# Four-layer fp32 attention and FFN kernel on one core: five engine queues in another order, and weight-piece waits on the last products

## The reference, cut to what matters

```python
x = x + L0_xattn(layernorm(x), ctx)      # softmax(q k^T) of the context with itself, then tokens times it
x = L0_ffn(x)                            # residual + ternary-weight FFN, int8 activations, hidden 1024, silu gate
x = x + L1_xattn(layernorm(x), ctx)      # 16 heads of 128, 8 key/value heads, Wo
x = x + L1_ffn(layernorm(x))             # fp8-rounded weights, inner 768, silu(gate) * up, then down
```

## Time and profile before

| what | us |
|---|---|
| median of three runs | 320.16 (319.19 to 320.66) |
| the profiled execution, whole | 319.45 |
| its span, first to last instruction | 317.4 |
| around the span | 2.05 |
| mean granted TensorE clock, of full speed | 0.993 |

### The profile page before, as it was taken

How to read it: one execution, slowest core, us unless ns; L and a number is a source line. 1 busy time by engine, 2 the same in 40 slices (tenths; PEclk the granted TensorE clock), 3 DMA queues, 4 the chain that set the end, 5 groups by cost and what they waited for, 6 DMA issues and landing times.

```text
span 317.4 us, 6401 instructions
## 1 busy us (share of the span) xinstructions
PE 294.9 (93%) x1981; PEld 258.8 (82%) x1992; DVE 252.2 (79%) x713; ACT 258.5 (81%) x607; POOL 217.9 (69%) x290
## 2 busy tenths in 40 slices
PE   3676999999999999999989999999999999999994
PEld 2465566889988987899779989889999998989784
DVE  3789698989888789888889788897877595766674
ACT  0869796489999989999997897788899998975350
POOL 3786663566887788797877897878897696772001
PEclk9999799999999999999999999999999999999999
DMA  7994602002046867678637566687665466200201
GB/s 219 380 350 135 176 0 68 1 1 76 5 81 179 245 168 199 165 209 202 180 88 207 150 179 162 165 221 203 147 188 151 116 197 200 69 2 0 68 1 66
DMA packets 54609, 44.59 MB, mean 140 GB/s; under 512 B 11696, under 2 KB 45104, under 8 KB 54576
## 3 DMA queue, kind: packets, MB, share of 16 engines
q1 hardware_dynamic: 54016, 43.93, 49.1%
q10 hardware_dynamic: 560, 0.26, 0.3%
HBM read 27.01 MB, written 15.20 MB: 133 GB/s over the span
## 4 chain that ended last, share of the span: by engine, by line
PE 21%; ACT 15%; POOL 8%; issue 5%; DVE 1%; ACTq 0%; POOLq 0%; DVEq 0%
PE pb L2015 14%; PE pb L2278 4%; ACT sm L980 4%; POOL tp_lo L666 4%; ACT pT_hi L992 3%; PE pb L2312 2%; POOL xn L588 1%; ACT sm L998 1%; ACT L980 1%; POOL sm L661 1%; ACT L1019 1%; ACT fuse L1019 1%; ACT q_hi L975 1%; ACT oT_hi L1004 1%; POOL rstd L582 1%
## 5 line engine op out<-in xcount | busy, mean ns | idle before, releaser
L666 POOL TENSOR_TENSOR tp_lo<-tp,pT_hi 128x512 fp32r<-128x512 f32 x54 | 69.2, 1297 | 20.9 <-ACT pT_hi L992 20.8
L980 ACT ACTIVATE sm<-sm,smin 128x256 f32<-128x256 f32 x128 | 63.6, 503 | 1.1 <-DVE smin L1563 0.7
L1563 DVE CUSTOM_DVE_ANT_0 sm<-pb,mask_all 128x256 f32<-128x256 f32 x128 | 47.5, 419 | 4.0 <-PE pb L2015 3.6
L1580 DVE STREAM_TRANSPOSE blocks<-sm 128x1024 f32<-128x1024 f32 x27 | 33.5, 1240 | 7.0 <-DMA block_room<-blocks 6.1
L2015 PE MATMUL pb<-ctx_hi,q_hi 128*128 128x256 f32 x128 | 37.8, 295 | 0.5 <-DVE q_lo L1550 0.4
L2015 PE MATMUL pb<-xT_hi,m_hi 128*128 128x256 f32 x128 | 37.2, 291 | 0.1
L2015 PE MATMUL pb<-n_hi,oT_hi 128*128 128x256 f32 x128 | 37.1, 290 | 0.1
L2015 PE MATMUL pb<-xT_hi,m_lo 128*128 128x256 f32 x128 | 36.2, 283 | 0.0
L2015 PE MATMUL pb<-xT_lo,m_hi 128*128 128x256 f32 x128 | 36.2, 283 | 0.0
L2015 PE MATMUL pb<-ctx_hi,q_lo 128*128 128x256 f32 x128 | 36.2, 282 | 0.0
L2015 PE MATMUL pb<-ctx_lo,q_hi 128*128 128x256 f32 x128 | 36.1, 282 | 0.0
(11 more groups left out here) (195 smaller groups left out, 946.4 us busy)
## 6 DMA issues: line engine op xcount, KB each, us to landing
block_room<-blocks SPq DMA_DIRECT2D x108, 128.0 KB, 2.5
tp<-block_room SPq DMA_DIRECT2D x54, 256.0 KB, 3.1
w_raw<-in_w SPq DMA_DIRECT2D x4, 576.0 KB, 4.2
wraw<-in_wgvT SPq DMA_DIRECT2D x4, 512.0 KB, 7.4
wraw<-in_woutT SPq DMA_DIRECT2D x2, 512.0 KB, 10.6
out<-xb SPq DMA_DIRECT2D x4, 256.0 KB, 2.2
xa<-in_x SPq DMA_DIRECT2D x3, 256.0 KB, 4.6
xb<-in_ctxT SPq DMA_DIRECT2D x2, 256.0 KB, 6.1
```

The lines of the kernel that those rows point to most:

```text
L666: g.tensor_tensor(tp_lo[:, z, c, :], tp[:, z, c, :], as_f32(pT_hi[:, c, :]), ALU.subtract).then_inc(pT_lo_pool, 1)
L980: a.activation(sm[:, n % 2, k, :], sm[:, n % 2, k, :], ACT.Exp, bias=smin[:, n % 2, k:k + 1], scale=-1.0, accum_out=ssum[:, n % 2, k:k + 1 ...
L1563: v.tensor_tensor_reduce(out=sm[:, n % 2, k, :], in0=bank(passing_bank("s", 2 * n + h))[:, (k % 2) * S:(k % 2 + 1) * S], in1=mask_all[:, b ...
L1580: v.transpose(blocks[:].rearrange("p g k b -> p k g b"), sm[:, n % 2, :, :].rearrange("p k (g b) -> p k g b", b=32)).then_inc(blocks_done, 1)
```

## The change

The set of calls on each queue is the same before and after; only their order differs (and the banks in `PASSING`, rewritten to match), beside one edit of waits in `down`. The core of the diff, queue by queue:

```diff
@@ SP @@
             rows(2)
+            gate_value(1)
             rows(3)
             gate_value(0)
             gate_value(2)
-            gate_value(1)
             gate_value(3)
             contexts(1)
             hidden_out(0)
+            raw(5)
             raw(0)
+            scales()
             norm_weight()
+            raw(4)
             mask_bytes()
-            raw(4)
-            raw(5)
+            raw(3)
             raw(6)
+            hidden_out(1)
             raw(1)
-            hidden_out(1)
-            raw(3)
             raw(8)
...
             blocks_read(19)
-            eighth(3)
-            scales()
             blocks_read(20)
@@ POOL @@
             outputs_split(0)
-            ternary_out(5)
             integers(0)
             integers(1)
+            ternary_out(5)
             rows3(0)
...
-            normalise(21)
             rows3(3)
             probs_low(18, 0)
             probs_low(18, 1)
+            normalise(21)
             rows4(1)
...
             probs_low(29, 1)
+            eighths_out(14)
             normalise(31)
-            rows4(2)
             eighths(15)
             eighths_out(15)
+            rows4(2)
             rows4(3)
             output(2)
@@ ACT @@
+            context_high(0)
             projected1(0)
-            context_high(0)
             values_high(0)
+            sums(0)
             rows1(0)
             exps1(0)
             projected1(1)
-            sums(0)
             sums(1)
...
             probs(10, 1)
             outputs(9)
             silu(6)
+            gate_copy(7, 1)
             queries(15)
-            gate_copy(7, 1)
-            normalise(13)
-            silu(7)
             outputs(10)
             probs(11, 0)
             exps(14, 0)
...
+            queries(16)
             probs(12, 0)
-            queries(16)
             probs(12, 1)
+            silu(7)
             queries(17)
             normalise(15)
             exps(16, 0)
...
             probs(31, 0)
             probs(31, 1)
+            fuse_high(3)
+            gate4_silu(5)
             outputs(31)
             fuse_high(4)
-            gate4_silu(5)
@@ DVE @@
             centred(0)
-            inverse1(2)
             added1(1)
-            ternary(3)
             scaled(0)
             weight_sums(1)
+            inverse1(2)
+            ternary(3)
             second_stats(1)
@@ PE @@
             def down(c, n):
                 h, i = divmod(c, KI)
                 pe.wait_ge(f_lo_done, c + 1)
+                if c < KI:
+                    pe.wait_ge(w8_done, -(-(2 * KD * INNER + (i + 1) * D) // PIECE))
                 if c == 0 and n == 0:
-                    pe.wait_ge(w8_done, B * EIGHTS)
...
             gate_half(0, 0)
             gate_half(0, 1)
-            gate_half(1, 0)
+            mix(2)
             value_half(0, 0)
...
             attn_out(30, 1)
+            down(2, 1)
             attn_out(31, 0)
             attn_out(31, 1)
+            down(3, 1)
+            rows4(2)
             up4(5)
-            rows4(2)
-            down(3, 1)
             down(0, 0)
```

More of the change, by code:

```diff
@@ L752, in _ @@
             normalise(9)
+            probs_low(7, 0)
             eighths(3)
             eighths_out(3)
-            probs_low(7, 0)
             probs_low(7, 1)
+            eighths(4)
+            probs_low(8, 0)
             normalise(10)
-            probs_low(8, 0)
             probs_low(8, 1)
@@ L763, in _ @@
             probs_low(9, 0)
-            eighths(4)
             eighths_out(4)
+            probs_low(9, 1)
             normalise(12)
-            probs_low(9, 1)
             eighths(5)
@@ L778, in _ @@
             eighths_out(6)
+            normalise(15)
             probs_low(12, 0)
@@ L781, in _ @@
             eighths(7)
-            normalise(15)
+            eighths_out(7)
             probs_low(13, 0)
@@ L836, in _ @@
             normalise(27)
+            eighths(14)
             probs_low(25, 0)
@@ L1112, in _ @@
             exps(2, 1)
-            normalise(1)
+            fused_queries(7)
             outputs(0)
@@ L1116, in _ @@
             probs(1, 1)
-            rounded(2)
+            normalise(2)
+            exps(3, 0)
             queries(4)
-            normalise(2)
+            exps(3, 1)
+            probs(2, 0)
             rounded(3)
-            exps(3, 0)
-            probs(2, 0)
-            exps(3, 1)
+            outputs(1)
             probs(2, 1)
+            queries(5)
+            normalise(3)
+            gate_copy(4, 0)
             exps(4, 0)
-            queries(5)
             exps(4, 1)
-            outputs(1)
-            normalise(3)
+            outputs(2)
             normalise(4)
-            gate_copy(4, 0)
-            gate_copy(4, 1)
             exps(5, 0)
@@ L1135, in _ @@
             queries(6)
+            normalise(5)
+            gate_copy(4, 1)
             silu(4)
-            normalise(5)
-            outputs(2)
             gate_copy(5, 0)
@@ L1141, in _ @@
             queries(7)
-            gate_copy(5, 1)
             probs(3, 1)
+            rows3(1)
             exps(6, 0)
-            rows3(1)
             exps(6, 1)
             outputs(3)
+            probs(4, 0)
             normalise(6)
-            probs(4, 0)
+            exps(7, 0)
+            queries(8)
+            exps(7, 1)
             probs(4, 1)
-            queries(8)
-            exps(7, 0)
-            exps(7, 1)
             normalise(7)
             queries(9)
+            gate_copy(5, 1)
             exps(8, 0)
@@ L1199, in _ @@
             probs(10, 0)
+            normalise(13)
             probs(10, 1)
@@ L1223, in _ @@
             probs(13, 0)
+            exps(16, 1)
             probs(13, 1)
-            exps(16, 1)
+            outputs(12)
+            exps(17, 0)
+            queries(18)
             normalise(16)
-            queries(18)
-            exps(17, 0)
-            outputs(12)
+            outputs(13)
+            probs(14, 0)
             exps(17, 1)
-            probs(14, 0)
             probs(14, 1)
-            outputs(13)
             normalise(17)
@@ L1300, in _ @@
             exps(26, 1)
+            gate4_copy(2)
             gate4_silu(0)
+            probs(23, 0)
+            outputs(22)
+            gate4_silu(1)
+            queries(28)
             normalise(26)
-            queries(28)
-            gate4_copy(2)
-            probs(23, 0)
-            gate4_silu(1)
-            outputs(22)
+            probs(23, 1)
             gate4_silu(2)
-            probs(23, 1)
             exps(27, 0)
             exps(27, 1)
+            queries(29)
+            fuse_high(0)
             probs(24, 0)
@@ L1314, in _ @@
             probs(24, 1)
-            fuse_high(0)
+            gate4_copy(3)
             exps(28, 0)
-            queries(29)
             exps(28, 1)
-            gate4_copy(3)
             normalise(27)
-            normalise(28)
             probs(25, 0)
@@ L1324, in _ @@
             queries(30)
+            normalise(28)
             outputs(24)
@@ L1327, in _ @@
             exps(29, 1)
-            gate4_silu(3)
             probs(26, 0)
-            outputs(25)
             probs(26, 1)
             normalise(29)
+            gate4_silu(3)
+            outputs(25)
             exps(30, 0)
-            exps(30, 1)
+            queries(31)
             probs(27, 0)
             probs(27, 1)
-            queries(31)
+            outputs(26)
+            exps(30, 1)
+            gate4_copy(4)
+            fuse_high(1)
             normalise(30)
-            outputs(26)
-            gate4_copy(4)
+            probs(28, 0)
+            fuse_high(2)
+            probs(28, 1)
+            gate4_copy(5)
             outputs(27)
-            probs(28, 0)
-            probs(28, 1)
             gate4_silu(4)
-            fuse_high(1)
-            fuse_high(2)
-            gate4_copy(5)
             probs(29, 0)
@@ L1355, in _ @@
             normalise(31)
-            fuse_high(3)
             outputs(29)
@@ L1973, in _ @@
             probs_low(30, 1)
+            eighths(15)
             outputs_low(29)
@@ L2322, in _ @@
             rows1(1)
+            rows1(2)
             probs(0)
@@ L2328, in _ @@
             project1(3)
-            turn_kv(0)
+            energy(2)
             probs(1)
-            energy(2)
             mix(1)
             energy(3)
+            turn_kv(0)
             turn_kv(1)
-            rows1(2)
+            integers(0)
             turn_kv(2)
+            probs(2)
+            weight_sum(1)
             turn_kv(3)
-            integers(0)
-            weight_sum(1)
-            probs(2)
-            mix(2)
             gate_half(0, 0)
             gate_half(0, 1)
-            gate_half(1, 0)
+            mix(2)
             value_half(0, 0)
@@ L2396, in _ @@
             fuse_qk(6)
+            turn_queries(7)
+            queries(2)
+            fuse_vo(7)
             fuse_qk(7)
@@ L2418, in _ @@
```

(39 more changed lines are left out.)

628 lines of the change are left out of this document (313 added, 315 removed), and 49 rows, old and new, of the table PASSING.

## The result

The kernel after takes **322.01 us** (median of 12 runs, 320.26 to 325.70) against 320.11 for the kernel before beside it (12 runs, 318.66 to 320.88): ratio **1.0061**, 95% interval 1.0037 to 1.0086. It is slower by 0.6%. The forecast was 318.3, faster by 0.6%; the range 314.8 to 322.8 holds the time, the direction is wrong. The profiled execution took 322.79 us, 320.8 of it span. Medians in this document are of all runs, ratios and the counts of runs by clock only of those that are not slow: the one of 325.70 us here is slow, and so are one of 417 and one of 487 us among the experiments.

The account below looks back on a forecast made before the run. PE, busy 93%, was taken as the bound, leaving only its 22.5 us of idle time to win. Terms -0.3 - 0.9 - 1.0 + 0.3 = -1.9 us, from the median 320.16, gave 318.3 us; range 314.8 to 322.8.

Parts of the forecast that it names:

- Waits of `down`: Lower-half `down` products wait for 12 to 16 weight pieces, not all 16; priced 0, ends -0.2 to +1 us.
- First table load: At the start, ACT's table load runs under PE's first products, so `qk` starts 1.3 us earlier, near 7.5 us.
- Loads: Early `scales()` delays `hidden_out(1)` by 1 to 2 us, taking back the table's gain: net -0.3, ends -1.3 and +1.5.
- the larger gain: Rival, 315 us: table load not taken back, no half-speed stretch, loop saves half a microsecond, -5 us; chance 0.13.
- Gate halves: `gate_half(0, 0)` and `(0, 1)` fill PE's 1.78 us hole before `mix(2)`: -0.9 us, ends -1.8 and 0.
- `silu(7)`: Leaving the chain before PE's `tp_lo` wait at 162.21 us: -1.0; its second visit with two more table loads: +0.3.
- Small moves: Some 300 small order moves, not priced one by one: taken as 0, ends -2 to +4 us.
- the broken hand-off of `tp_lo`: Rival, 323 us: POOL's later `normalise` turns PE's 8 waits for `tp_lo` into 16, +4.8 us; chance 0.21.

Follow-up runs that it names:

- late before: Orders of the kernel after up to about 66 us, but `scales()` left late, those of the kernel before behind, with `down`'s piece waits: 319.58 us, 0.9990.
- late after: The kernel after with one call moved, `scales()` back to its late place ahead of `blocks_read(20)`: 319.14 us, 0.9991.
- part 1: The kernel before with only the edit of `down`'s waits: 320.06 us, 1.0013.
- the kernel of part 3: The kernel before with one call moved, `context_high(0)` first on ScalarE, ahead of `projected1(0)`: 318.12 us, 0.9943.
- a badly cut experiment: Two kernels joining the orders of before and after at about 66 us: early before with late after 323.68 us, 1.0116; early after with late before 319.58, 0.9990.
- the last kernel of part 9: The kernel before with `context_high(0)` first on ScalarE and the first two gate halves ahead of `mix(2)`, in banks drained early: 318.04 us, 0.9947.

## Why the prediction was wrong

The runs give the change a ledger, in ratios to before. The early table load: 0.9943. The rest of the early order, without `scales()`: the kernels with late before (0.9990) and with late after (0.9991) both stand 0.5% above it, the waits of `down` included. The late order, some 300 moves: those two differ by 0.01%, so nothing, within 0.3% (their early calls are the same but for a few at the cut). `scales()` early: 0.9991 to 1.0061, plus 0.7%. Sum: -0.6 + 0.5 + 0.0 + 0.7 = +0.6%. It closes because each step is the difference of two measured kernels, some timed at different times, so each is good to about 0.3%.

Against the forecast, in us by these ratios: table load and loads -0.3 forecast, +0.4 measured (+1.5 by the medians); the rest of the early order with the gate halves -0.9, measured +1.5; the late order with `silu(7)` -0.7, measured 0. Two steps failed, the price of the loads and the nothing put for the early small moves, beside the gate halves that won nothing.

- *Waits of `down`, 0*: right (part 1). The last `w8r` was written by 287.93 us, and `down(0, 0)` came behind 292.45.
- *First table load, 1.3 us*: right, 1.3 by the medians and 1.8 by the ratio, and not eaten up.
- *Loads, "1 to 2 us of delay", net with the table load -0.3*: **this step failed.** The mechanism was the right one, down to the calls: `scales()` in front of `hidden_out(1)`, DVE's `inverse1(2)` behind `weight_sums(1)`, the third softmax and mix behind that. The hold was 1.7 us, inside the estimate of 1 to 2. But I let it take back the table's 1.3 us and no more. Measured it is 2.2 to 2.9 us: 1.4 to 1.7 at full clock, and the rest with the clock, which had no term of its own. I had costed the stretch at half speed at 1.7 us and asked only whether the change could remove it, under the larger gain, not whether a later landing could lengthen it, to 6.9 us in the trace.
- *Gate halves, -0.9*: wrong; nothing (0.9947 against 0.9943). The hole was real, but filling it moved the mix by 0.66 us (32.03 against 31.37), and what the gates gained the mix and its followers gave back. The end named for it was 0, and 0 it was. That the bank could hold them was not priced at all, and it decides between 0 and +2.3 us (+1.6 among runs at a clock of 0.996 or more).
- *`silu(7)`, -1.0 and +0.3*: the wait for `tp_lo` near 162 did go, and comes back when the call goes back, but no gain is left. The second pair of loads cost about what the first wait had. The table loads at 168.72 and 172.46 are followed by the next function 1.29 us later, and the call ahead runs up to each, so the drain that the Trainium skill counts ("ScalarE: Activation LUTs", What ACT_TABLE_LOAD costs) is again not seen.
- *Small moves, 0*: right as a sum, in the loop. Of the early part **this step failed**: its moves cost 0.5% together, 1.5 us, inside the ends of -2 to +4 but put at nothing because no row priced them. It is not clock alone: at 0.996 or more the kernels with them have 319.6 and 318.8 us, the table load alone 318.1. One of them shows in the traces, DVE's `inverse1(2)` behind `weight_sums(1)`, which I had named and priced only through the loads. In the kernel after with `scales()` late POOL's third softmax still waits for it and starts 2.7 us later than in the kernel of part 3 (25.53):

```profile
28.23 1.29 POOL L607 TENSOR_SCALAR pr<-pr,erec 128x256 f32<-128x256 f32 x2 [1.63 <-DVE erec L1431]
```

The third mix behind it starts at 32.46 instead of 31.37. That move was never run alone, so how much of the 1.5 us it carries is not shown.

- Of the rivals, the broken hand-off of `tp_lo` gave a time near the right one for the wrong reason: its waits fell from 4.8 to 3.2 us.

My first theory after the result, the early part, was right in its place and half refuted by a badly cut experiment; the second, three waits of the loop, is not borne out. What stays open: how the 0.5% divides among the other early moves (the order of the first loads, of the raw weights, of ACT's sums and of DVE's `inverse1(2)` all changed), and why the clock falls in more runs of one order than of another, since no run held it.

The gate halves added nothing to it (318.04 us, 0.9947): the kernel before with `context_high(0)` first, **318.12 us (0.9943)**, is as good as any here, and one line away from before.

## What to carry to other kernels

Price a small load by what it holds in the queue, not by its bytes, and look at what waits behind the last of the weights that it goes ahead of; a load that is needed at 200 us has no business ahead of one that is needed at 28. Where a stage has a stretch at a lower clock, give the clock a term of its own in the sum, with both signs, and compare the granted clock of each run beside its time: runs at full clock alone tell what the order itself costs. When a kernel is cut from two orders, list the calls that the cut leaves on the wrong side before believing the result, and look for waits at the seam that neither parent has.

## What the runs showed of the hardware

A load that reads one 1 KB row 128 times held the loads behind it by 1.7 us for 128 KB, 77 GB/s; in the kernel before the queue moved 395 GB/s from 19 to 22 us. The Trainium skill ("DMA: Bandwidth & Descriptors", Anatomy of one DMA) gives the part of a load's time that depends on its size as bytes over 436 GB/s, for loads of the gpsimd path. This one goes by SP's queue; at that rate it would by estimate hold the queue for 0.3 us, and the measurement decides. Packets of 24 bytes, 256 of them, held it for 0.1 us, within the spread between traces.

The granted clock differs between runs of the same kernel, and the share of runs under 0.996 differs between orders: 10 of 11 of the kernel after, 0 of 8 of the last kernel of part 9. It differs between rounds of timing too, for the kernel before from 6 of 35 to 13 of 20. In the kernel after the clock falls to half speed at 30.5 us in a slice with PE busy 5.02 of 8 us, in before at 33 us behind one of 5.17; in the kernel of part 3 the same quiet (4.93 of 8 us from 24 to 32) went by at full clock, so the quiet is not enough to foretell it.
